# Low parts from a PSUM copy, and TensorE's four tiles as a loop of two passes over two

## What is computed

```python
e = jnp.stack([tbl_0[ids[:, 0]], ..., tbl_25[ids[:, 25]]], axis=1)      # 512 x 26 x 128
combined = jnp.concatenate([e, r_dense_x[:, None, :]], axis=1)
z = jnp.einsum('bfd,bgd->bfg', combined, combined)[:, _TRIU_I, _TRIU_J]  # 351 pairs
h = jnp.concatenate([z, r_dense_x], axis=1)
h = jnp.maximum(h @ W_top1 + b_top1, 0.0)                                # 479 x 512
h = jnp.maximum(h @ W_top2 + b_top2, 0.0)                                # 512 x 256
y = h @ W_top3                                                           # 256 x 1
```

## Time and profile before

| | us |
|---|---|
| median of 3 runs | 110.68 |
| lowest and highest | 109.79, 111.02 |
| the profiled execution | 111.06 |
| its span, first to last instruction | 109.2 |
| TensorE busy, matmuls | 99.5 (91%) |
| VectorE, ScalarE, GpSimd busy | 57.2, 34.6, 68.6 |

### The profile page before, as it was taken

How to read it: one execution, slowest core, us unless ns; L and a number is a source line. 1 busy time by engine, 2 the same in 40 slices (tenths; PEclk the granted TensorE clock), 3 DMA queues, 4 the chain that set the end, 5 groups by cost and what they waited for, 6 DMA issues and landing times.

```text
span 109.2 us, 3405 instructions
## 1 busy us (share of the span) xinstructions
PE 99.5 (91%) x1532; PEld 84.6 (77%) x1532; DVE 57.2 (52%) x113; ACT 34.6 (32%) x59; POOL 68.6 (63%) x72
## 2 busy tenths in 40 slices
PE   6995999999998999999899699999999899756992
PEld 6993888887875887888688599879987798655980
DVE  0069999999999999970200731071204530061130
ACT  5016336708416043222520520153412244201022
POOL 3778777777787787777776777777777760000000
PEclk9999999999999999999999999999999999997699
DMA  2999999656968992112212112212122111000000
GB/s 57 194 381 395 364 388 370 245 186 211 376 228 245 392 305 59 48 54 62 59 53 56 48 50 75 56 48 54 48 75 56 50 48 30 0 6 6 0 0 4
DMA packets 6001, 14.68 MB, mean 134 GB/s; under 512 B 1889, under 2 KB 2913, under 8 KB 5858
## 3 DMA queue, kind: packets, MB, share of 16 engines
q1 hardware_dynamic: 3938, 10.26, 27.1%
q0 software_dynamic: 2048, 4.20, 13.4%
HBM read 14.45 MB, written 0.00 MB: 132 GB/s over the span
## 4 chain that ended last, share of the span: by engine, by line
PE 49%; DVE 36%; DMA 7%; ACT 3%; issue 2%; SPq 1%; DVEq 0%
DVE onehot L470 19%; PE gram_ps L310 13%; PE look_ps L341 11%; DVE low L460 10%; PE look_ps L275 8%; PE look_ps L351 7%; DMA table<-tbl_dram 7%; PE turn_ps L296 5%; DVE dots L478 4%; DVE pairs L492 3%; PE look_ps L321 2%; PE look_ps L333 2%; ACT high L545 1%; PE look_ps L360 1%; ACT vecs L554 1%
## 5 line engine op out<-in xcount | busy, mean ns | idle before, releaser
L254 POOL DMA_INDIRECT rows<-tbl_dram,ids_rows x64 | 67.7, 1058 | 20.4 <-issue 19.2
L275 PE MATMUL look_ps<-onehot,high 128*128 128x512 f32 x88 | 33.7, 401 | 1.4 <-ACT high L545 1.2
L275 PE MATMUL look_ps<-onehot,low 128*128 128x512 f32 x88 | 32.9, 392 | 0.1
L470 DVE TENSOR_SCALAR onehot<-ids_wide,row_ids 128x1024 fp32r<-128x1024 int32 x44 | 30.0, 742 | 5.4 <-DMA ids_wide<-ids_look_dram 5.4
L275 PEld LDWEIGHTS look_ps<-onehot,high 128*128 128x128 f32 x88 | 16.3, 188 | 6.0 <-DVE onehot L470 2.2
L275 PEld LDWEIGHTS look_ps<-onehot,low 128*128 128x128 f32 x88 | 16.5, 188 | 3.8 <-DVE low L460 0.6
L478 DVE STREAM_TRANSPOSE dots<-gram_ps 128x352 f32<-128x352 f32 (+2 forms) x12 | 5.6, 466 | 19.8 <-PE gram_ps L310 19.8
L545 ACT CAST high<-table 128x1024 fp32r<-128x1024 f32 (+1 forms) x10 | 11.3, 1138 | 14.7 <-DMA table<-tbl_dram 14.7
L565 ACT COPY vecs<-turn_ps 128x512 f32<-128x512 f32 x16 | 9.4, 594 | 15.1 <-PE turn_ps L296 15.1
L310 PE MATMUL gram_ps<-vecs 128*27 128x27 f32 x1024 | 12.8, 195 | 1.5 <-ACT vecs L565 0.7
L341 PE MATMUL look_ps<-pairs_t,w_sb 128*128 128x128 f32 x96 | 13.5, 297 | 0.2 <-ACT pairs_t L571 0.2
(11 more groups left out here) (34 smaller groups left out, 49.6 us busy)
## 6 DMA issues: line engine op xcount, KB each, us to landing
table<-tbl_dram SPq DMA_DIRECT2D x6, 512.0 KB, 9.9
ids_wide<-ids_look_dram SPq DMA_DIRECT2D x5, 512.0 KB, 5.1
table<-tbl_dram SPq DMA_DIRECT2D x4, 640.0 KB, 4.9
rows<-tbl_dram,ids_rows POOLq DMA_INDIRECT x64, 4.3
w_sb<-w_dram SPq DMA_DIRECT2D x1, 1024.0 KB, 9.2
w_sb<-w_dram SPq DMA_DIRECT2D x1, 512.0 KB, 7.8
x_rows<-x_dram SPq DMA_DIRECT2D x1, 256.0 KB, 10.5
ids_rows<-ids_gather_dram SPq DMA_DIRECT2D x1, 32.0 KB, 1.9
```

The source lines that it names most:

```text
L254: nc.gpsimd.indirect_dma_start(rows[:, t * NG + i, :], None, tables[GATHER_FIELDS[i]], bass.IndirectOffsetOnAxis(ap=ids_rows[:, t * NG + i ...
L275: mm = nc.tensor.matmul(look_ps[:, j % 2 * 2 + f, :], weights, onehot[:, (STEP0[j] + k) % RING, f * BATCH:(f + 1) * BATCH], start=(name == ...
L470: nc.vector.tensor_scalar(onehot[:, q % RING, :], ids_wide[:, j % WIDE_HELD, :], row_ids[:, kind(j), k:k + 1], None, ALU.is_equal).then_in ...
```

## The change

Two parts. In the lookups, ScalarE, having rounded a table from the third on, copies up to 8 chunks of the high part into gram_ps, once the low part of the table before is made; VectorE subtracts this copy from the table. The last two chunks of tables of 10 are subtracted as before, by a second instruction. There is one such place in PSUM.

In the tile stage, TensorE's code is a loop of two passes, each over two tiles. For this, rows and vecs hold two tiles; what the lookups give for tiles 2 and 3 is saved to a new buffer, known, and ScalarE copies it into vecs when the gram of the tile two before is done (place_known, 11 vectors of 128 samples). The saves of the lookups are therefore two instructions each, first the two tiles at hand. GpSimd's gathers for tiles 2 and 3 wait, four at a time, for the turn that frees their rows. Waits in the loop compare with an expression of the pass number, and layer1_dense reads at an offset that depends on it. A pass turns the rows of its second tile (turn_second) and of the next pass's first (turn_next), in the second pass stale rows. In front of the last turn of a pass's second tile stand three waits for gathers that were begun, each with three matmuls on zeros. The warm-up is 8 matmuls on zeros in the code (16 in the profile) instead of 17 (34), and the other keep_clock calls are gone. The order of tile work on TensorE is new: no gram of the next tile is set into a tile's waits.

```diff
-CODE_SHIFT = 9
+FIRST_COPIED = 2
+COPY_CHUNKS = 8
+HELD = 2
+PASSES = TILES // HELD
+FILLERS = 3
...
-        rows = sb("rows", [P, TILES * NG, D])
+        rows = sb("rows", [P, HELD * NG, D])
...
-        vecs = sb("vecs", [P, BATCH // 2, SLOTS, 2])
+        vecs = sb("vecs", [P, HELD * P // 2, SLOTS, 2])
+
+        known = sb("known", [P, (BATCH - HELD * P) // 2, NL + 1, 2])
...
+        def copied(i):
+
+            return gram_ps[:].rearrange("p b (k d) -> p (b k) d", d=D)[:, 0:min(CHUNKS[i], COPY_CHUNKS), :]
...
             for t in range(TILES):
+                h = t % HELD
                 for i in range(NG):
+                    if t >= HELD and i % GROUP == 0:
+
+                        pool.wait_ge(turned, turn_index(t - HELD, i // GROUP) + 1)
...
+            def keep_clock():
+
+                for _ in range(FILLERS):
+                    nc.tensor.matmul(gram_ps[:, 0, 0:4 * SLOTS], zeros[:], zeros[:, 0:4 * SLOTS],
+                                     start=True, stop=True)
+
+            def turn_second(r, g):
+
+                pe.wait_ge(turn_saved, r * (HELD * NGROUPS) + turn_index(1, g) - 1)
+                if g == NGROUPS - 1:
+
+                    for i in range(1, GROUP):
+                        pe.wait_ge(gather_begun, r * GROUP + i)
+                        keep_clock()
+                pe.wait_ge(rows_landed[1][g], r * (16 * GROUP) + 16 * GROUP)
+                turn(turn_index(1, g), 1, g)
+
+            def turn_next(g):
+
+
+                pe.wait_ge(turn_saved, turn_index(2, g) - 1)
+                pe.wait_ge(rows_landed[0][g], PASSES * (16 * GROUP))
+                turn(turn_index(2, g), 0, g)
...
+            with pe.Fori(0, PASSES) as r:
+
+                pe.wait_ge(look_saved, r + COUPLES)
+                pe.wait_ge(turn_saved, r * (HELD * NGROUPS) + turn_index(1, 0))
+                gram(0, 0)
+                layer1_dense(r, 0)
+                turn_second(r, 0)
+                gram(0, 1)
+                turn_second(r, 1)
+                turn_pairs(r, 0, 0)
+                turn_pairs(r, 0, 1)
+                layer1_pairs(r, 0, 0)
+                turn_pairs(r, 0, 2)
+                layer1_pairs(r, 0, 1)
+                layer1_pairs(r, 0, 2)
+                turn_second(r, 2)
+                layer2(r, 0, 0)
+                layer2(r, 0, 1)
+                turn_second(r, 3)
+                layer3(r, 0)
+
+                pe.wait_ge(look_saved, r * 2 + COUPLES)
+                pe.wait_ge(turn_saved, r * (HELD * NGROUPS) + turn_index(2, 0))
+                gram(1, 0)
+                gram(1, 1)
+                layer1_dense(r, 1)
+                turn_pairs(r, 1, 0)
+                turn_next(0)
+                layer1_pairs(r, 1, 0, 0, 1)
+                turn_pairs(r, 1, 1)
+                layer1_pairs(r, 1, 0, 1, N1)
+                turn_pairs(r, 1, 2)
+                layer1_pairs(r, 1, 1)
+                layer1_pairs(r, 1, 2)
+                turn_next(1)
+                layer2(r, 1, 0)
+                layer2(r, 1, 1)
+                turn_next(2)
+                layer3(r, 1)
+                turn_next(3)
...
+                dve.wait_ge(high_copied, i - FIRST_COPIED + 1)
+                n = min(CHUNKS[i], COPY_CHUNKS)
+                ins = subtract(part(low, i)[:, 0:n, :], part(table, i)[:, 0:n, :], copied(i))
+                if n < CHUNKS[i]:
+                    ins = subtract(part(low, i)[:, n:, :], part(table, i)[:, n:, :], part(high, i)[:, n:, :].bitcast(F32))
+                ins.then_inc(low_ready, 1)
...
                 copy(part(high, i), part(table, i)).then_inc(high_ready, 1)
+                if i >= FIRST_COPIED:
+
+                    if i > FIRST_COPIED:
+                        act.wait_ge(low_ready, i)
+                    act.wait_ge(high_ready, i + 1)
+                    n = min(CHUNKS[i], COPY_CHUNKS)
+                    copy(copied(i), part(high, i)[:, 0:n, :].bitcast(F32)).then_inc(high_copied, 1)
...
+            def place_known(t):
+
+                act.wait_ge(gram_done, t - HELD + 1)
+                act.wait_ge(known_saved, 1)
+                act.wait_ge(last_look_saved, 2)
+                at = (t - HELD) * P // 2
+                copy(tile_vecs(t, slice(0, NL + 1)), known[:, at:at + P // 2]).then_inc(look_saved, 1)
```

More of the change, by code:

```diff
@@ L156, in build @@
         x_landed, w1_landed, w2_landed, small_landed = sem("x_landed"), sem("w1_landed"), sem("w2_landed"), sem("small_landed")
-        rows_landed = [[sem(f"rows_landed{t}_{g}") for g in range(NGROUPS)] for t in range(TILES)]
+        rows_landed = [[sem(f"rows_landed{h}_{g}") for g in range(NGROUPS)] for h in range(HELD)]
+        gather_begun = sem("gather_begun")
         blank = sem("blank")
@@ L281, in look_up @@
                     if j == COUPLES - 1 and f == 1 and name == "low" and k % 2 == 1 and k < 2 * NGROUPS:
-                        turn(0, k // 2)
+                        pe.wait_ge(turn_saved, turn_index(0, k // 2) - 1)
+                        pe.wait_ge(rows_landed[0][k // 2], 16 * GROUP)
+                        turn(turn_index(0, k // 2), 0, k // 2)
             def turn_x():
@@ L362, in layer3 @@
                 mm.then_inc(y_done, 1)
-            def keep_clock(count):
-                for _ in range(count):
-                    nc.tensor.matmul(look_ps[:, 1, 0:P], zeros[:], zeros[:], start=True, stop=True)
             pe.wait_ge(zeros_ready, 1)
-            for b in range(2):
-                for q in range(0, QB, 4):
-                    nc.tensor.matmul(gram_ps[:, b, q * SLOTS:(q + 4) * SLOTS], zeros[:], zeros[:, 0:4 * SLOTS],
-                                     start=True, stop=True)
-            for _ in range(CODE_SHIFT):
-                nc.tensor.matmul(gram_ps[:, 0, 0:4 * SLOTS], zeros[:], zeros[:, 0:4 * SLOTS], start=True, stop=True)
+            for _ in range(2 * QB // 4):
+                nc.tensor.matmul(look_ps[:, 2, 0:4 * SLOTS], zeros[:], zeros[:, 0:4 * SLOTS], start=True, stop=True)
             look_up(0)
@@ L456, in _, with subtract @@
             copy = nc.vector.tensor_copy
+            def subtract(out, a, b):
+                return nc.vector.tensor_tensor(out, a, b, ALU.subtract)
             def make_low(i):
-                dve.wait_ge(high_ready, i + 1)
-                nc.vector.tensor_tensor(part(low, i), part(table, i), part(high, i).bitcast(F32), ALU.subtract
-                                        ).then_inc(low_ready, 1)
+                if i < FIRST_COPIED:
+                    dve.wait_ge(high_ready, i + 1)
+                    subtract(part(low, i), part(table, i), part(high, i).bitcast(F32)).then_inc(low_ready, 1)
+                    return
+                dve.wait_ge(high_copied, i - FIRST_COPIED + 1)
[4 more added lines that the diff above has]
+                ins.then_inc(low_ready, 1)
             def make_hot(j, k):
@@ L566, in save_turn, with save_pairs @@
                      turn_ps[:, n % 2, :].rearrange("p (s b o) -> p b s o", s=GROUP, o=2)).then_inc(turn_saved, 1)
-            def save_pairs(t):
-                for c in range(2):
-                    act.wait_ge(pairs_turned, t * PAIR_CHUNKS + c + 1)
-                    copy(pairs_t[:, c, :], turned_pairs(c)).then_inc(pairs_saved[0], 1)
+            def save_pairs(t, c):
+                act.wait_ge(pairs_turned, t * PAIR_CHUNKS + c + 1)
+                copy(pairs_t[:, c, :], turned_pairs(c)).then_inc(pairs_saved[0], 1)
             def save_h1(t):
```

193 lines of the change are left out of this document (71 added, 122 removed).

## The result

| | before | after |
|---|---|---|
| median of 4 runs, us | 110.24 | 120.44 |
| lowest and highest | 109.62, 111.02 | 119.83, 121.14 |
| the profiled execution, and its span | 111.06, 109.2 | 119.83, 118.0 |
| first gram starts | 54.36 | 57.44 |
| tile stage, to the last copy of y | 53.0 | 58.75 |

The ratio is 1.092, 95% interval 1.082 to 1.103: slower, and more so than the 114.9 forecast; the range ended at 120.0. Every ratio here compares the undisturbed executions alone, since some executions of any kernel run a few per cent longer at a lower granted clock, so it can differ from the ratio of the medians. Of the 8.8 us that the span grew, 3.1 lie in the lookups and 5.75 in the tile stage.

A forecast was written before the change was run, and what follows sets the result against it. VectorE was taken to bind the lookups, TensorE the tile stage. From the profiled 111.06 us, +2.7 for lookups and +1.5 for tiles gave 115.3, or 114.9 at the median's level; range 109.6 to 120.

The forecast's parts named there:

- Lookups: First stage: copy waits and splits +2.35, shorter warm-up +0.6, split saves -0.28, together +2.7 us.
- The four waits: Lookups: VectorE waits 0.45 us for ScalarE's copy before tables 3, 5, 7 and 9, 1.8 in all.
- rival (d): Lookups: subtract with one PSUM operand takes 0.74 us for 1.21; total 110.3, or 108.4 with one standstill less; chance 0.16.
- (b): Lookups keep their time, VectorE's waits falling where TensorE is late anyway; total 112.2 us; chance 0.16.
- Second pass: Tile loop's second run: 27.4 us, less 1.1, plus 0.3, less 1.8 for quick grams, plus 0.2: 25.0.
- correction (1): Second pass: code may already be on the engine, so its two tiles' grams take 2.56 us, not 3.46; -1.8.
- Rival (a): Tile loop: code is fetched again, second pass pays standstill, slow grams, branch wait, slow clock; 122.2 us, or 120; chance 0.14.
- First pass: Tile loop's first run: 27.4 us, plus 1.9 for a standstill, plus 0.2: 29.5.
- correction (2): First pass: a gram of 256 matmuls in one piece, as in tile 3, brings the same standstill; +1.9 us.
- the price list: Tile loop: pieces priced from before's rows, first tile 14.9 us and second tile 12.5, a pass 27.4.
- (c): Tile loop: code quick in both passes, no standstill, all grams at 2.56 us; total 111.2; chance 0.16.
- The gathers: GpSimd: eight long gathers some 4 us shorter in all, buying nothing; last lands near 89.5, TensorE reaches it near 95.

## Why the prediction was right, and where it failed

**Lookups, +2.7 forecast, +3.08 measured.** Right in kind and nearly in size. The copies cost 2.44 (57.44 against 55.00 without them; forecast 2.35). The short warm-up makes the last lookup 0.68 later without them, 53.82 for 53.14 (forecast 0.6). The split saves gave back 0.04 and not 0.28: from the start of the last lookup to the gram it is 1.18 for 1.22. The four waits were 0.42, 0.36, 0.91 and 0.42 where I had 0.45 each. The 0.91 is a wait I had not looked for: ScalarE rounds table 7 only at 31.51, since its DMA lands late. Its row, then that of the copy:

```profile
31.51 1.27 ACT L564 CAST high<-table 128x1280 fp32r<-128x1280 f32 x1 [2.13 <-DMA table<-tbl_dram]
32.87 1.02 ACT L571 COPY gram_ps<-high 128x1024 f32<-128x1024 f32 x1
```

The subtract's price (1.21) and the copy's (1.05 forecast, 1.018) held, so rival (d) fell; (b) fell with the later lookups. The reading behind the subtract was loose, since 0.691 for 512 elements and 1.21 for 1024 are not one rate (1.35 and 1.18 ns an element). The low clock at 9 us is read from the pace (0.42 from matmul to matmul, 9.13 to 12.48 for eight, against 0.23 later); the windows' column says 1.00 there, because the trace names a level only from the first change on, which is at 12.23.

**Second pass, forecast 25.0 (27.4 less 1.1, plus 0.3, less 1.8 for quick grams, plus 0.2), measured 24.9.** The total is right, in part by luck. Its gram halves take 1.28, and the two stretches with its grams are 0.2 shorter than forecast (3.95 and 2.28 for 3.89 and 2.56); the stretch with the fillers, 100.23 to 105.73, took 5.5 for 5.1; register waits and branch show nothing: from the end of a turn to the gram it is 0.66 in before, 0.66 here. What was wrong is the reason for the quick grams, correction (1), "in the second pass it may be on the engine already" (1,384 instructions, for the 1,450 estimated). New code had quick grams too, 1.27 in the second pass written out, and code on the engine had slow ones beside gathers, 1.81 in the loop without copies and fillers. They were quick because GpSimd's last gather, at 87.13, lay ahead of the pass. Rival (a) fell outright. The page after lists seven blocks, the last of them ended at 87.4, and the window of the second pass shows a DMA share of 0.00. The rule of the Trainium skill that I had set beside it (Runtime: NRT & Kernel Launch, "Instruction fetch mechanics"), that a taken branch out of the two-page window forces a fetch, does not hold here: the branch went back over 1,384 instructions and nothing was fetched. The same section gives TensorE room for 2048 instructions; with that figure the trace agrees, and I had passed over it; no run has a longer loop, so the limit itself is not shown.

**First pass, forecast 29.5 (27.4, plus 1.9, plus 0.2), measured 33.8.** This is the step that failed: correction (2), "The first pass has a gram of 256 matmuls in one piece, as tile 3 had: +1.9 for the same standstill". Three standstills came, 3.4 us in all (+1.5 over the forecast). A slow stretch came behind the second, which I had priced at 1.7 in the rival but set at nothing in the sum (+1.4, from the turn at 65.15 to the end of the first layer 6.46 for 5.02). The remaining 1.4 is smaller sizes: 0.8 in the pieces around the standstills (to 65.15, 5.45 without them for 4.79; the gram at 77.11, 3.64 for 3.46), and 0.8 in the price list, less 0.2 of register waits that did not come. In the list the stretch with the fillers took 5.5 for 5.1, and that from 81.87 to the next pass 9.4 for 9.0. The slow grams of 1.73 themselves were in the forecast, from before's rows. I had looked at the one standstill of before and taken it as a property of the last gram, when the question was how many instructions TensorE uses up between two places 256 apart. Two things of the change made that worse, and I costed neither as code. The shorter warm-up took 36 instructions out in front (CODE_SHIFT, nine products of full precision), which puts place 451 just inside the loop: with the places 40 further on, the first two standstills are gone, though no run shows that the pass is shorter for it. And the new order puts the two gram halves of a pass's second tile in one piece, 512 instructions that are 2.35 us of work; before, only the last tile had that. There the third standstill stays in every run of the new order.

**The sum.** 115.3 for the profiled execution, plus 0.4 (lookups), plus 4.3 (first pass), less 0.1 (second pass) gives 119.9; it was 119.83. (c) was half right: quick grams, but in one pass only, the one behind the gathers.

**The gathers** went as said: 1010 ns for 1058 in the mean (3.1 us in all, for the 4 forecast), the last issued at 87.13 and not 88.84, and TensorE never waited for rows. That the gathers took less time bought nothing: even the 88.84 of before lies ahead of the second pass, which begins at 91.28 and so has its quick grams.

What stays open: why a gather makes TensorE pause; what places would be better for the kernel before; and what brings a slow stretch. One kernel had three standstills and no slow stretch, and in the profile of the one with 40 more instructions a stretch began at 66.84 with no standstill for code ahead of it in the tile stage, only waits of 0.97 and 0.58 for the pairs.

## What to carry to other kernels

Count TensorE's instructions against time, not only their durations: where TensorE stood still for new code here, 256 of them took 3.2 to 4.0 us from place to place, and matmuls of 27 columns, two instructions each, use them in 1.3; where the places 256 apart fall in such a stretch decides what it costs, so padding taken out in front moves them. A loop body that stays on the engine runs its second pass without standstills for code, so a loop pays from the passes after the first, and with two passes the first must not be made worse. Before a quick second pass is put down to the loop, look at what else has ended by then: here it was the gathers that had slowed the grams. A copy made to relieve one engine needs a second place to land in, or the engine that it should relieve waits for it.

## What the runs showed of the hardware that I had not expected

- A loop of 1,384 TensorE instructions, 5.4 blocks, was run a second time without fetching any; written out, the same work fetched five blocks more and took 31.9 us for 24.9.
- New code reached TensorE one block of 256 instructions at a time: in eleven standstills of six kernels, 0.9 to 1.6 us from passing the place before until the block began, 0.9 to 1.5 for its packets, 1.2 to 1.5 until TensorE went on. Where TensorE waited ahead of a place, the block could begin before the place was passed (92.68 for 93.82 in the kernel before).
- TensorE's matmuls of 27 columns pause for about 0.2 us, 0.4 after the start of a gather on GpSimd and 0.1 before it, whether the code is new (first pass) or on the engine (second pass of the loop without copies and fillers): 128 of them took 1.81 us beside gathers and 1.28 without.
- VectorE subtracts with one operand in PSUM at the rate of two in SBUF: 1.214 us for 1024 elements, 0.674 for 512. ScalarE copies 1024 elements from SBUF to PSUM in 1.018.
- A slow stretch of 3.41 us after a standstill costs about 1.5 us, though it need not come: with the fillers taken out, there was none.
